# A transformer layer with 4-bit grid feed-forward: first and last slots of the schedule written anew

## The reference

```python
def xattn(y, Z, ...):
    y = layernorm(y + attention(y, y, y, causal=True)) * g1 + beta1
    y = layernorm(y + attention(y, Z, Z, causal=False)) * g2 + beta2
    ff = relu(y @ w1 + b1) @ w2 + b2            # 256 -> 1024 -> 256
    return layernorm(y + ff) * g3 + beta3

def ffn(x, w_gate, w_up, w_down):               # 256 -> 704 -> 256
    q = fp4_quant_dequant                       # blocks of 16: scale = max|x| / 6, then the grid 0, .5, 1, 1.5, 2, 3, 4, 6
    h = silu(q(x) @ q(w_gate).T) * (q(x) @ q(w_up).T)
    return q(h) @ q(w_down).T

x = x + xattn(layernorm(x), ctx, ...)
x = x + ffn(layernorm(x), w_gate, w_up, w_down)
```

## Time and profile before

| | us |
|---|---|
| Runs of the kernel before: median (lowest, highest) of 3 | 603.36 (601.0, 606.66) |
| Profiled execution: its time | 602.97 |
| Profiled execution: span, first to last instruction | 601.1 |
| PE busy / DVE busy | 565.8 / 497.5 |
| POOL busy / ACT busy | 386.6 / 373.5 |

### The profile page before, as it was taken

One profiled execution on the slowest core, in us unless ns is written; L12 is line 12 of the kernel. 1 busy time (PEld: TensorE's weight loads), 2 busy tenths in 40 slices (PEclk: granted clock), 3 DMA queues, 4 the chain that ended last, 5 costly groups with the idle time before them and its releaser, 6 DMA issues.

```text
span 601.1 us, 12447 instructions
## 1 busy us (share of the span) xinstructions
PE 565.8 (94%) x4043; PEld 537.7 (89%) x4043; DVE 497.5 (83%) x1220; ACT 373.5 (62%) x777; POOL 386.6 (64%) x466
## 2 busy tenths in 40 slices
PE   4697789999999999999999999999999999999888
PEld 3486689999999999999999999999999999999787
DVE  4969978888888988888988888887978878887885
ACT  3655576667758585766768575766667574756232
POOL 3667656686657666676667667676757656666543
PEclk9978999999999999999999999999999999999979
DMA  7701001010101001010101001010101010000000
GB/s 227 241 2 36 1 2 45 1 55 1 61 2 42 14 1 62 0 52 0 61 0 52 0 18 43 0 52 0 61 1 36 2 36 1 19 2 19 0 10 27
DMA packets 18743, 19.30 MB, mean 32 GB/s; under 512 B 1537, under 2 KB 18193, under 8 KB 18705
## 3 DMA queue, kind: packets, MB, share of 16 engines
q1 hardware_dynamic: 18704, 18.82, 10.0%
HBM read 14.62 MB, written 4.19 MB: 31 GB/s over the span
## 4 chain that ended last, share of the span: by engine, by line
PE 76%; issue 5%; DVE 5%; POOL 5%; ACT 2%; POOLq 0%; DVEq 0%; ACTq 0%
PE R L1112 6%; PE R L1114 6%; PE R L1113 6%; PE TR L1017 5%; PE O L1164 5%; PE R L1182 4%; PE R L1184 4%; PE R L1183 4%; PE O L1227 4%; PE O L1229 4%; PE O L1228 4%; PE O L1206 3%; PE O L1208 3%; PE O L1207 3%; PE R L1017 3%
## 5 line engine op out<-in xcount | busy, mean ns | idle before, releaser
L461 POOL TENSOR_TENSOR rs<-mv,neg_half 128x1 f32<-128x1 f32 (+1 forms) x112 | 69.0, 626 | 28.7 <-DVE mv L1573 27.4
L1112 PE MATMUL R<-gu_hi,xqT_hi 128*128 128x352 f32 x240 | 80.2, 334 | 1.8 <-issue 0.9
L1182 PE MATMUL R<-y2T_hi,w_hi 128*128 128x256 f32 x256 | 76.8, 300 | 2.7 <-DVE y2T_lo L1701 1.3
L754 ACT ACTIVATE hqT_hi<-R 128x768 fp32r<-128x768 f32 x29 | 23.6, 813 | 86.8 <-PE R L1017 86.8
L1114 PE MATMUL R<-gu_hi,xqT_lo 128*128 128x352 f32 x240 | 77.3, 322 | 0.0
L1113 PE MATMUL R<-gu_lo,xqT_hi 128*128 128x352 f32 x240 | 77.2, 322 | 0.0
L1227 PE MATMUL O<-w_hi,hT_hi 128*128 128x256 f32 x256 | 74.4, 291 | 0.0
L1184 PE MATMUL R<-y2T_hi,w_lo 128*128 128x256 f32 x256 | 72.4, 283 | 0.0
L1183 PE MATMUL R<-y2T_lo,w_hi 128*128 128x256 f32 x256 | 72.4, 283 | 0.0
L1229 PE MATMUL O<-w_hi,hT_lo 128*128 128x256 f32 x256 | 71.8, 281 | 0.0
L1228 PE MATMUL O<-w_lo,hT_hi 128*128 128x256 f32 x256 | 71.8, 280 | 0.0
(11 more groups left out here) (195 smaller groups left out, 1839.5 us busy)
## 6 DMA issues: line engine op xcount, KB each, us to landing
x_in<-in_x SPq DMA_DIRECT2D x16, 256.0 KB, 2.7
x_res<-in_x SPq DMA_DIRECT2D x16, 256.0 KB, 2.7
out<-x SPq DMA_DIRECT2D x32, 128.0 KB, 1.8
ctx_rows<-in_ctx SPq DMA_DIRECT2D x16, 64.0 KB, 2.5
hT<-in_L_xattn_w SPq DMA_DIRECT2D x1, 1024.0 KB, 7.8
hh<-in_L_xattn_w SPq DMA_DIRECT2D x1, 768.0 KB, 8.5
wd_raw<-in_L_ffn_w_down SPq DMA_DIRECT2D x1, 704.0 KB, 8.5
w_raw<-in_L_ffn_w_gate SPq DMA_DIRECT2D x1, 640.0 KB, 4.5
```

The lines of the kernel that those rows point to most:

```text
L1112: mm(o, xh, gu_hi[:, c, m, cols], start=(c == 0), stop=False)
L1182: mm(o, w1_hi[:, c, cols], y2T_hi[:, c, :], start=(c == 0), stop=False)
```

## The change

Line numbers in the diff are those of each file. In words:

- **Queue of transfers (SP).** The second half of x is loaded right behind the first and the small columns, ahead of `w_gate`, the context and `beta1`; before it came behind them.
- **PE, first waits.** `keep_warm(6)` ahead of the transpose of the columns, `keep_warm(9)` ahead of `turn_y0(0, 0)` and twice `keep_warm(2)`: float32 matmuls of 128 columns whose result is overwritten or never read. `keep_busy(TR[1][:], 2)` ahead of `values(1, 0, 0)`.
- **Heads of all engines.** The stages of units 1 and 2 come earlier in every queue, the weight groups later: group 1's `w_lift`/`w_drop` stand behind the first cross-attention, group 1's transpose (`w_turn(1)`) behind all of `ff1(1, 0)` and not ahead of it, group 3's behind `ff2`. `w_lower(3)` moves into slot 3, `w_lower(4)` there ahead of the norm of x, `w_turn(5)` ahead of `ff1`'s third quarter with the relus of the first half done earlier on ACT. The wait on two low parts in `ready_for_scores` is gone, since no group has been turned into those banks by then.
- **Tail.** The last unit's `x_norm` (DVE) becomes `last_shift` (DVE, one column) and `last_norm` (ACT, 256 columns). `scale_x(b, g, 1)` goes ahead of `unscale_h(b, g, 1)` on POOL, `turn_xq(b, h, 1)` ahead of `split_turn`, part 1's scale on DVE and POOL ahead of the rows of tile 0; the 14 and 8 `keep_busy` become 17, 6 and 6.

```diff
@@ SP
+            load_x(0, 1, 1)
             load_ffn(w_gate, 0, gate_in)
...
             load_row(beta1, beta1_row, beta1_in)
-            load_x(0, 1, 1)
@@ PE
+            def keep_warm(count):
+
+                for _ in range(count):
+                    mm(bank(0)[:, 0:P], ident[:], ident[:], start=True, stop=True)
+
             pe.wait_ge(ident_set, 1)
+            keep_warm(6)
             pe.wait_ge(cols_in, 16 * 5)
...
-                if n == 2:
-                    pe.wait_ge(wq_lo, 2)
...
             def head():
+                keep_warm(9)
                 turn_y0(0, 0)
+                keep_warm(2)
                 scores(0, 0)
+                turn_y0(0, 1)
                 turn_context(0)
+                keep_warm(2)
                 values(0, 1, 0)
                 values(0, 1, 1)
...
+                keep_busy(TR[1][:], 2)
                 values(1, 0, 0)
                 values(1, 0, 1)
+                fold_b1(2)
                 turn_z2(1, 0)
-                w_turn(1, 0, 2, 1)
...
                 cross_values(1, 0)
-                w_turn(2, FC // 2, 0, 0)
+                w_turn(1, FC, HEAD, 1)
                 ready_for_ff2(1, 0)
...
                 turn_context(1)
+                w_turn(2, FC, 0, 0)
+                ff2(1, 0, 1, range(FC))
                 w_turn(3, FC, HEAD, 0)
-                ff2(1, 0, 1, range(FC))
@@ PE, slot
+                if isinstance(b, int) and HALVES * b + h == Q:
+                    w_turn(5, FC + FC // 2, 0, 0)
                 if q1:
                     down(b, h - 1, 1)
                 if f:
                     ff1(b, h, (4, 5))
                 if q:
-                    if isinstance(b, int) and HALVES * b + h == Q:
-                        w_turn(5, FC + FC // 2, 0, 0)
                     turn_xq(b, h, 0)
@@ PE, tail
-                keep_busy(TR[1][:], 14)
+                keep_busy(TR[1][:], 17)
...
+                wait(pe, h_set, b, h, Q, 2 * T, 1)
+                keep_busy(bank(0), 6)
+                turn_xq(b, h, 1)
                 split_turn(b, g)
-                turn_xq(b, h, 1)
...
-                keep_busy(bank(2), 8)
+                keep_busy(bank(2), 6)
@@ ACT
+            def last_norm(b, h, t):
+                wait(act, ln_rstd[4], b, h, F, T, t + 1)
+                act.wait_ge(ln_shift[4], t + 1)
+                act.activation(xn[:, t, :], x1[(h - F) % 2][:, t, :], ACT.Identity, bias=nm[4][:, t:t + 1],
+                               scale=rs[4][:, t:t + 1]).then_inc(ln_out[4], 1)
@@ DVE
+            def last_shift(b, h, t):
+                wait(dve, ln_rstd[4], b, h, F, T, t + 1)
+                v.scalar_tensor_tensor(nm[4][:, t:t + 1], mv[4][:, t:t + 1, 0], -1.0, rs[4][:, t:t + 1],
+                                       ALU.mult, ALU.mult).then_inc(ln_shift[4], 1)
...
-                x_norm(b, g, 0)
+                last_shift(b, g, 0)
@@ DVE, slot
                 if isinstance(b, int) and HALVES * b + h == Q:
+                    w_lower(3)
                     w_lift(5)
                     w_drop(5)
...
+                if isinstance(b, int) and HALVES * b + h == Q:
+                    w_lower(4)
                 if a:
                     self_reciprocal(b, h, 1)
@@ POOL, tail
+                scale_x(b, g, 1)
                 unscale_h(b, g, 1)
-                scale_x(b, g, 1)
```

More of the change, by code:

```diff
@@ L838, in slot @@
                 if f:
[L839 removed]
+                    if not early:
+                        relu(b, h, (0, 1))
                     relu_upper(b, h, (0,))
@@ L1262, in turn_context, with keep_busy @@
                 last.then_inc(ctx_turned, 1)
+            def keep_busy(o, count):
+                for _ in range(count):
+                    mm(o, w1_hi[:, 0, 0:P], w1_hi[:, 0, 0:4 * P], start=True, stop=True)
             def turn_y0(b, h):
@@ L2060, in head @@
                 aggregate(0, 0, 2, 0, 1)
+                w_lower(0)
+                w1_lower(1)
+                shift(0, 0, 2, 0, (0, 1))
+                y2T_lower(1, 0)
                 self_part(1, 0, 0)
```

191 lines of the change are left out of this document (90 added, 101 removed).

## The result

| kernel | median us (lowest to highest, runs) | ratio to before, 95% interval |
|---|---|---|
| before | 603.56 (601.0 to 606.66, 13) | |
| changed | 606.54 (604.77 to 608.46, 13) | 1.0042 [1.0025, 1.0060] |

The changed kernel is slower by 3.0 us, half a per cent; I had said 596.0, faster by 7. The profiled execution of it took 604.77, which is the lowest of its 13, so its trace tells less than the whole loss: its span is 602.7 for 601.1.

A forecast was written before the change was run, and what follows sets the result against it. It took PE to bound the middle, DVE's queue order the head, and a chain from engine to engine the end. 602.97 - 5.0 (head) - 2.4 (tail) = 595.6 profiled; median 0.39 above: 596.0, range 592.5 to 599.5.

The forecast's parts named there:

- Steps 1 and 2: Head's start: warm matmuls give scores 1.3 and values 1.5 us less; z1's norm at 16.2, cross_max(0, 1) at about 20.1.
- the clock brings nothing: Rival, chance 0.17: recorded clock is right early or pace falls again in new waits; head gives -0.6, total 602.8.
- Steps 3 and 4: Head: cross_sum(0, 1) at 23.4 for 30.78; values(1, 0) at full clock, y2T_lower(1, 0) at 29.8, 9.7 us earlier.
- step 5: Head: cross_max(1, 0) at 39.6 for 52.38, 12.8 us earlier; PE's wait of 3.77 us goes.
- Step 6: Head, weight chain: w_lift(2) at about 48.9, 8.3 us later; y2T_lower of slot 3 at 64.4, 3.1 of 12.8 us left.
- the weight chain sets the end: Rival, chance 0.11: w_lift(2) up to 9.7 us later than forecast, gate_up at 89.5, total 605.0; head even at 54.6.
- The bound that I gave for stretching: Head: DVE operations beside long POOL ones can stretch, 2 to 3 us for three or four such meetings.
- Step 7: Slot 3: w_lower(4) at 69.9, PE hardly waits and keeps its clock, gate_up at 79.8 for 85.50, 5.7 us.
- The risk that I named: Tail: last_shift could be held by a POOL product of 1.39 us, 0.6 us more than before instead of 0.65 less.
- 1.4 us by scale_x ahead of an unscale_h: Tail, second half: scale_x ahead of a 1.4 us unscale_h helps start turn_xq(1) and the second last_gate_up 2.4 us earlier.
- their starts move by 2.2 to 2.7: Tail, last parts in DVE's queue: starts 2.2 to 2.7 us earlier, last sum 2.5; 2.4 taken, bounds 0 to 4.

The follow-up runs named there:

- the clock kept: The changed kernel with unread matmuls in PE's waits from 16 us to slot 3: 602.94 us, ratio 0.9998 to the kernel before.
- the weight chain mended: New heads with unread matmuls, old tail, weight chain earlier, w_drop(3) and maxima ahead of first ff_sum, seven more matmuls ahead of ff2: 600.07 us (0.9945).
- the run with 8 matmuls in its tail: The changed kernel with both of DVE's tail orders put back and 8 unread matmuls for 6 ahead of part_turn: 605.16 us (1.0033).
- the mended new tail: The changed kernel with DVE's, POOL's and ACT's tail orders put back: 603.18 us (1.0007); with the last norm on DVE too, 603.25 (1.0001).

## Why the prediction was wrong

The forecast lies 10.5 us from the median. In the profiles the head gave nothing (gate_up 0.4 us later) where I had summed a gain of 5.0, and the tail lost 1.0 where I had a gain of 2.4; falls of the clock in executions that the profile does not show are the likely rest. The steps that failed are the full clock in steps 3, 4 and 7, the idle time of DVE that the first reading took for granted, the wait at gate_up that I did not see, and two terms of the tail.

**Steps 1 and 2** held: scores and `values` ran at full pace (L1178, six records in 1.47 us for 2.94), z1's norm at 16.05 for the 16.2 forecast, cross_max at 20.66 for 20.1. The rule of the page "TensorE: Matmul & The Clock Gate" of the Trainium skill (section "What's actually happening"), that the throttled state is the default and activity releases it, fits here, and the first half of the rival "the clock brings nothing", that the recorded clock is right for the first microseconds, fell. Little of it reached the end, though: the warm matmuls alone left the time as it was.

**Steps 3 and 4** failed first, on the words "at full clock takes 3.1 us for 14 records". I took PE at full pace once it had been woken, and priced the falls only for `ff2`, at 1.5 us. The same section of the Trainium skill has another side that I did not carry on: the throttled state comes back when activity ends. The trace agrees, with waits of 1.03 to 2.73 us ahead of the falls, and the change, by moving work out from in front, left PE waiting there. `values(1, 0)` began at 27.04 in the middle of a fall. With the clock kept, y2T_lower comes at 31.70 for 33.45 and cross_max(1,0) at 41.36 for 44.15. So of the 4.6 us by which step 5 was late, the clock is 2.8, by one profile of each kernel; the two unfilled profiles with a shorter early fall agree (cross_max(1,0) at 41.6). That was my rival "the clock brings nothing", in its second form, the pace that falls again in the new waits.

**Step 6** was right in mechanism and in length: from w_lift(2) to y2T_lower of slot 3 I counted 15.5 us, it took 15.8. It started 4.8 us late because steps 3 to 5 were late, 53.67 against the 54.6 from which, I had said, the head is even; and the head was even. So the rival "the weight chain sets the end" named the right place with the wrong cause: it had ACT's order, and the clock was 2.5 of the 4.8 us (51.14 with it kept). For the other 2.2 no run names a cause. But what I inferred from it was too strong: the runs with the chain 6 us earlier gained under 2.

**What lies under all of it** is the first reading: "the head is thus bound by the order of DVE's queue". It rested on waits of PE behind weight work, and on DVE at 9.04 of 10 us, which I read as order and should have read as load. DVE is 82% busy from 10 us to gate_up; moving its instructions about brings some stages sooner and others later. My account is that the end moves only by the waits that vanish, less the stretching that appears; the sums of busy and idle time fit it, and no run isolates it. I had summed 5.7 us of gain without asking which of DVE's 13.5 idle microseconds would go. The bound that I gave for stretching, 2 to 3 us, stood in the range and not in the sum. In the changed kernel these rows of DVE are longer than the same shape elsewhere, each beside a product on POOL (0.96, 0.41, 0.63, 0.95 and 0.20 us otherwise):

```profile
16.86 2.13 DVE L1545 SCALAR_TENSOR_TENSOR ha<-ha,hs 128x768 f32<-128x768 f32 x1
...
45.92 1.60 DVE L1583 TENSOR_TENSOR shift_parts<-shift_row,shift_parts 1x256 fp32r<-1x256 f32 x1
...
48.09 1.72 DVE L1672 TENSOR_TENSOR hT_lo<-hT,hT_hi 128x512 fp32r<-128x512 f32 x1
...
56.40 1.66 DVE L1539 SCALAR_TENSOR_TENSOR hs<-ha,hs 128x768 f32<-128x768 f32 x1
...
61.08 1.21 DVE L1527 TENSOR_SCALAR h_div<-h_amax 128x88 f32<-128x88 f32 x1
```

The kernel before has such rows too, at other places (`w2_lower(0)` 3.05 us, in the changed kernel 1.75). If each single row of DVE from 10 us to xqT_lo is taken against the shortest of its shape in these traces, the stretch adds up to about 10.3 us before and 12.9 after. The new order did not bring stretching in, it brought 2.6 us more of it. For one row a run settles the cause. With the weight chain mended POOL has no product running beside `shift_parts`, and the same instruction takes:

```profile
41.05 0.42 DVE L1594 TENSOR_TENSOR shift_parts<-shift_row,shift_parts 1x256 fp32r<-1x256 f32 x1
```

For the others it is argued from the rows.

**Step 7** held in its shape: `w_lower(4)`, 69.9 by my count, came at 74.14, and from y2T_lower to gate_up it took 16.5 us for 15.4. I had said that PE hardly waits there and keeps its clock; it waited 2.73 and 1.76 us and ran at 0.50 from 66.8 to 73.4. It left PE a wait of 1.95 us at the end where there had been 0.85. I saw no wait there, and in most profiles the clock fell behind it, up to 1.5 us that my sum did not have.

**The tail.** The risk that I named is what happened: last_shift, one column, took 1.38 us beside POOL's product of 1.39, and 0.16 at the second tile, where no such product ran, as the page "GPSIMD Engine Reference" of the Trainium skill (section "Key points") has it for an instruction with two SBUF inputs. x_max came 0.56 us late, which is the 0.6 that I had priced for that case; the sum had it 0.65 early. But in the whole kernel the norm is worth nothing either way (603.25 and 603.18). Two terms were wrong. "1.4 us by scale_x ahead of an unscale_h" forgot what the moved unscale_h would now stand beside: x_lift took 1.15 for 0.42. And "their starts move by 2.2 to 2.7", the last parts, I had not walked through all queues: last_max and last_scale behind a low part that waits 1.25 us for ACT, abs_rows behind a silu that waits for PE. h_rec came 2.35 us later instead. Put back, the orders of DVE, POOL and ACT are worth 2.1 us by the ratios and 3.4 by the medians, and what then stays of the new tail gives 1 us at most, not 2.4.

## What to carry to other kernels

Before you reorder a stretch, add up busy and idle time of the engine that is busiest there: order can give back only its idle time, and a queue that is 82% busy, as here, may hand an early gain back at its end. Every wait that a change leaves on TensorE may cost clock behind it, so price the wait and what follows it, at half pace, and put unread matmuls into the waits that are already there before you move anything: here that alone gave some 4 us, where the change as it is lost 3. A profile of the fastest execution can leave out a loss that most executions have, and one of the slowest can show one that few have; compare the profiled time with the median first.

## What the runs showed that I had not expected

- A wait of 1.95 us in which TensorE does nothing (PE at gate_up) was followed by the clock at 0.50 for some 3 us in eight of the eleven profiles of new heads that have no filler there; with eight unread matmuls in it, in none of three. A wait of 0.85 us at the same place never was.
- The same kernel loses its clock for different lengths in different executions: the fall that began near 19 us lasted to 29.4 in the changed kernel's profile; in the run with 8 matmuls in its tail, whose head is the same, the clock read 0.63 from 24 to 28 us, y2T_lower came at 32.24 for 33.45 and gate_up at 83.92 for 85.92. One profile of each kernel therefore settles no difference under 2 us in the head.
- In the tail it is the same. Of eleven profiles with the new tail or its mended forms, four have the clock at 0.50 somewhere between 582 and 600 us. With the tail as changed it took 42.2 us with such a fall and 40.6 to 40.7 without (three profiles).
- A DVE instruction on one partition or one column can last nearly as long as the POOL product beside it: 1.60 us for 1x256 beside one of 1.82, 1.38 for 128x1 beside one of 1.39.
- Not tried: the old order with fillers together with the mended new tail. By the parts it would be up to 1 us under the best here by the medians, 0.2 by the ratios. The earlier load of x, which I had priced at nothing, was in no run by itself.
